# Two-layer graph network: 332 single-bucket edge tiles and 50 shared ones in place of 432, and the second layer in the edge loop's block

## Chip, cores, metric

The kernel runs on one core of a Trainium2 chip. The metric is the device time of one execution in microseconds (us). Engines: PE (TensorE), DVE (VectorE), ACT (ScalarE), POOL (GpSimd), SP (SyncE, which here only issues DMAs).

## The reference

1250 nodes with 512 features each, and 41250 directed edges (20000 random pairs in both directions, and one loop per node), sorted by destination. Everything is fp32.

```python
h = relu(layernorm(x))
m = relu(concat(h[src], h[dst]) @ W0.T + b)      # one row of 512 for each edge
x = x + segment_sum(m, src)                      # first layer
h = relu(layernorm(x))
msgs = (h @ W1.T)[src] * edge_weight[:, None]
out = segment_sum(msgs, dst)
x = x + where(out >= 0, out, alpha * out)        # second layer
```

## The kernel before

Nodes are split into ten blocks of 125 (`BN`), so an edge belongs to one of 100 buckets (source block, destination block). A *tile* is 128 edges of one bucket. Since the counts are only known on the chip, the number of tiles is the worst case: `MAXT = (E + 127 * 100) // 128 + 10 = 431`, in groups of four (`GRP`) 108 groups (`NGRP`) and 432 tiles (`NT`). Every engine works through all 432, empty ones too.

**First block: sorting, and the products of layer one.** The edges lie as 125 rows by 330 columns (`EROWS`, `ECOLS`). DVE counts the buckets (`hist`, `tiles_of`, `tile_base`), and in five chunks of 66 columns (`NCHUNK`, `CHUNK`) each edge gets its slot: PE counts by column (`count`), ACT copies the counts out (`copy_counts`), DVE scans them (`bases`), SP writes the sums as extra rows of `hot`, PE makes prefix sums (`prefix`), DVE picks each edge's own (`pick`) and `slots` works out tile, lane and table row. Then each column's edges are put where they belong in one of two ways: 136 columns by an indirect DMA that POOL issues (L374) to a table in DRAM; 194 columns by PE (`place`, L624): three matmuls of a 125x128 one-hot times value (`lane_piece`, by ACT L737 or DVE L459) with a 125x432 one-hot of the tile number (`hot_tile`, DVE L453). Between these columns PE also computes, from a written-out schedule (`STEP`, `TURN_AT`, ...), `a = h @ W0a.T + b` and `b = h @ W0b.T` for all ten blocks, each kept as a rounded high and a low part (`a_hi`, `a_lo`, `b_hi`, `b_lo`). The table is read back (`raw`), added to PE's part, and decoded to `local_s`, `local_d` (node number in its block) and `weight_h`, `weight_l`.

**Second block: the edge loop.** For each tile PE does four matmuls of 512 columns into one `edge_ps` (L994, L995, L999, L1000): `turned_d` with `b_hi`, `b_lo`, and `turned_s` with `a_hi`, `a_lo`. The turned one-hots are made by ACT, a group at a time, from a row that SP broadcasts from DRAM (`spread`): a Square (L1051) and a Relu (L1060). ACT writes `msg_hi` (L1076), DVE `msg_lo` (L1148), and PE sums both over the edges into `node_ps` (`sum_tile`, L955, L956); DVE adds each pair of tiles to `S` (L1129). For layer two the kernel builds a 1250x1250 matrix `M` of summed edge weights: DVE makes `hot_s`, `hot_d` of a group (L1139), POOL multiplies `hot_d` with the high and the low weights (L914), one PE matmul of 252 columns a tile gives a 125x125 block in both parts (`weights`, L966), ACT copies a pair out (L1068), DVE joins the parts (L1134), and POOL adds a block to `M` at an offset read from a table (L930). PE does two sums of an earlier tile behind the four edge matmuls of the next, so ACT and DVE have more than a tile's time. The loops run in turns of four groups (`UNROLL`) with register offsets.

**Third block: layer two.** It starts when all engines have ended the second. SP loads `W1` (L1242), DVE makes the statistics of all ten blocks of `S` (L1275, L1280), PE turns `h2` and `W1` (L1389, L1398), ACT and DVE split them into high and low parts, and PE computes `G = h2 @ W1.T` (ten blocks of 12 matmuls, L1379 to L1381) and `M` times `G` (ten blocks of 30). DVE does the last steps of each block (L1318, L1320, L1323) and SP stores it (L1245).

Of the kernel before, what the change touches and what calls it, by code (L numbers as in the profile page):

```python
# [20 lines left out]
ALU = mybir.AluOpType  # L21
ACT = mybir.ActivationFunctionType
# [22 lines left out]
MAXT = (E + (TILE - 1) * NBKT) // TILE + NBLK * (PAIR - 1)  # L45
NGRP = -(-MAXT // GRP)
NT = NGRP * GRP
# [26 lines left out]


# [3 lines left out]
UNROLL = 4  # L79
KC = D // P  # L80
# [6 lines left out]
assert 2 * NCHUNK == NBLK and (NGRP - 4) % UNROLL == 0 and UNROLL % 2 == 0  # L87


def build(nc, x, src, dst, edge_weight, w0, b0, w1, alpha, out):  # L90
    rows_dram = nc.dram_tensor("edge_rows", [2, NGRP, GRP * P], BF16).ap()
    table_dram = nc.dram_tensor("edge_table", [P * NT, TABLE_FIELDS], F32).ap()
    with ExitStack() as top:
# [8 lines left out]
        iota = sb("iota", [P, NT], F32)  # L102
# [6 lines left out]
        shift = sb("shift", [P, NBLK], F32)  # L109

# [5 lines left out]
        local_d = sb("local_d", [P, NT], F32)  # L116
        weight_h = sb("weight_h", [P, NT], F32R)
# [5 lines left out]
        with ExitStack() as early:  # L123
# [17 lines left out]
            tile_base = early_sb("tile_base", [EROWS, NBKT], F32)  # L141
            blk_small = early_sb("blk_small", [EROWS, 6, NBLK], F32)
# [11 lines left out]
        with ExitStack() as scope:  # L154
# [4 lines left out]
            digit_room = sb1("digit_room", [P, (2 * NBLK * ECOLS * 2 - 4 * NT * 4 - 2 * NGRP * (GRP + 2) * 4) // 4 + 32], F32)  # L159
# [14 lines left out]
            with ExitStack() as ranks:  # L174
                hot = sb1("hot", [EROWS + 2, NBKT, CHUNK], BF16, ranks)
            with ExitStack() as back:
                raw = sb1("raw", [P, NT, TABLE_FIELDS], F32, back)
                code = sb1("code", [P, NT], F32, back)
                spare = sb1("spare", [P, NT], F32, back)
                started = sb1("started", [NBKT, NT], F32, back)  # L180
            hot_room = sb1("hot_room", [P, NBKT * CHUNK], BF16)
            weight_all = raw[:, :, W_AT]
            iota_h = sb1("iota_h", [EROWS, P], F16)
# [11 lines left out]
            row_no = sb1("row_no", [EROWS, ECOLS], I32)  # L195
            bkt_small = sb1("bkt_small", [NBKT, 8], F32)
# [48 lines left out]
            carried = sem("carried")  # L245
            rows_in = sem("rows_in")
# [4 lines left out]
            slot_math = sem("slot_math")  # L251
# [26 lines left out]
            with nc.Block() as block:  # L278
                @block.sync
                def _(sp):  # L280
# [11 lines left out]
                    sp.dma_start(table_dram.rearrange("(p t) f -> p (t f)", p=P),  # L292
                                 zeros.rearrange("p t f -> p (t f)")).then_inc(cleared_dram, 16)
                    for k in range(NCHUNK):
                        for r, part in enumerate((base_hi, base_lo)):
                            sp.wait_ge(base_rows, 2 * k + r + 1)
                            sp.dma_start(hot[EROWS + r:EROWS + r + 1].rearrange("p (s d) c -> p s (d c)", s=NBLK),
                                         part.rearrange("s d c -> s (d c)")).then_inc(rows_in, 16)

                    for k in range(2):  # L300
# [3 lines left out]
                                 table_dram.rearrange("(p t) f -> p (t f)", p=P)).then_inc(table_in, 16)  # L304
# [4 lines left out]
                def _(pool):  # L309
# [7 lines left out]
                    pool.iota(iota[:], [[1, NT]], base=0, channel_multiplier=0,  # L317
# [65 lines left out]
                def _(dve):  # L383
# [46 lines left out]
                    def slots(k):  # L430
                        cols = slice(k * CHUNK, (k + 1) * CHUNK)
                        whole = planes[:, 0, :]
                        dve.wait_ge(picked, (k + 1) * NPICK)
                        dve.tensor_reduce(slot[:], planes.rearrange("p b c -> p c b"), AX.X, ALU.add).then_inc(slot_math, 1)
                        dve.wait_ge(slot_math, k * 4 + 1)
                        dve.tensor_scalar(whole, slot[:], -(TILE - 1) / 2, 1.0 / TILE, ALU.add, ALU.mult).then_inc(slot_math, 1)
                        dve.wait_ge(slot_math, k * 4 + 2)
                        dve.tensor_scalar(tile_no[:, k % 2, :], whole, MAGIC, -MAGIC, ALU.add, ALU.add).then_inc(slot_math, 1)
                        dve.wait_ge(slot_math, k * 4 + 3)
                        dve.scalar_tensor_tensor(out=lane[:, k % 2, :], in0=tile_no[:, k % 2, :], scalar=-float(TILE), in1=slot[:],  # L440
                                                 op0=ALU.mult, op1=ALU.add).then_inc(slot_math, 1)
                        dve.wait_ge(slot_math, k * 4 + 4)
                        dve.scalar_tensor_tensor(out=row_no[:, cols], in0=lane[:, k % 2, :], scalar=float(NT),
                                                 in1=tile_no[:, k % 2, :], op0=ALU.mult, op1=ALU.add).then_inc(slots_ready, 1)

                    def column(q):
# [6 lines left out]
                        dve.tensor_scalar(hot_tile[r][:], iota[0:EROWS, :], tile_no[:, k % 2, at:at + 1], None, ALU.is_equal)  # L453
                        if KINDS[k][at] == "A":
                            dve.tensor_scalar(hot_lane[r][:], iota_h[:], lane[:, k % 2, at:at + 1], None,  # L455
# [33 lines left out]

                    dve.wait_ge(dconst, 3)  # L490
# [8 lines left out]
                    dve.tensor_copy(iota_h[:], iota[0:EROWS, 0:P])  # L499
# [3 lines left out]
                    own(dve.tensor_scalar(zt[:], total_ps, (TILE - 1) / 2, 1.0 / TILE, ALU.add, ALU.mult))  # L503
                    own(dve.tensor_scalar(tiles_of[:], zt[:], MAGIC, -MAGIC, ALU.add, ALU.add))

# [4 lines left out]
                    own(dve.tensor_tensor_scan(pair_to, ones_row[:, 0:NBLK], pair_a, 0.0, ALU.mult, ALU.add))  # L510
# [10 lines left out]


                    own(dve.tensor_tensor(own_base[:], by_blk[0:NBLK],
# [5 lines left out]
                    for s in range(5, NBLK):  # L529
                        hot_of_block(0, s)  # L530
# [916 lines left out]
```

## Time before and its profile

| what | value |
|---|---|
| median of three runs | 1081.85 us (1081.13 to 1082.65) |
| the profiled execution: its time | 1083.92 us |
| the profiled execution: its span | 1082.2 us |
| granted TensorE clock, mean over the span | 0.987 |
| PE busy | 1023.7 us (95%), 4879 matmuls |
| DVE, ACT, POOL busy | 949.4, 836.0, 716.6 us |

The span is from the first to the last instruction, and the time is 1.7 us longer. Busy time of PE counts pipelined matmuls that overlap, so the distance between the starts of two matmuls is the better measure of its work.

### The profile page before, as it was taken

How to read it: one execution, taken by the hardware profiler on the slowest of the kernel's cores; microseconds unless marked ns; L12 is line 12 of the kernel's file. 1: busy time of each engine (PE TensorE's matmuls, PEld its weight loads, DVE VectorE, ACT ScalarE, POOL GpSimd, SP SyncE). 2: the span in 40 equal slices, each digit the busy share in tenths (PEclk: the TensorE clock that was granted, in tenths of full speed). 3: DMA queues.
4: the chain of work that ended last, by engine and by line, in shares of the span. 5: the costliest groups of instructions: out<-in, count | busy, mean ns of one | idle time of the engine just before them, and what ended most of it. 6: DMA issues, size and time to landing. Idle time of an engine off the chain costs nothing. (4 is left out here: it accounts for less than half of the span.)

```text
span 1082.2 us, 22605 instructions
## 1 busy us (share of the span) xinstructions
PE 1023.7 (95%) x4879; PEld 814.1 (75%) x4880; DVE 949.4 (88%) x1801; ACT 836.0 (77%) x1769; POOL 716.6 (66%) x1042
## 2 busy tenths in 40 slices
PE   5698999999799999999999999999999999959997
PEld 4386887777588788777888777777778877748775
DVE  7798899888599999999999999999999999973454
ACT  6777798788688888888888888888888888844210
POOL 3888787867567777777777777777777777730000
PEclk9999999999899999999999999999999999979999
DMA  7000000000111111111111111111111111010011
GB/s 209 2 2 3 2 3 2 4 2 2 54 44 43 42 43 39 43 41 41 44 38 43 42 43 43 38 43 42 42 43 38 43 42 42 25 39 1 20 34 42
DMA packets 37249, 38.15 MB, mean 35 GB/s; under 512 B 5990, under 2 KB 33431, under 8 KB 37212
## 3 DMA queue, kind: packets, MB, share of 16 engines
q1 hardware_dynamic: 32512, 37.07, 11.0%
q0 software_dynamic: 4416, 0.30, 1.6%
q8 instruction: 18, 0.29, 0.1%
q10 hardware_dynamic: 284, 0.33, 0.1%
q14 instruction: 19, 0.16, 0.0%
HBM read 34.04 MB, written 3.36 MB: 35 GB/s over the span
## 5 line engine op out<-in xcount | busy, mean ns | idle before, releaser
L1076 ACT ACTIVATE msg_hi<-edge_ps 128x512 fp32r<-128x512 f32 x432 | 257.8, 597 | 81.7 <-PE edge_ps L1000 81.7
L930 POOL TENSOR_TENSOR M<-M,pair_w 125x125 f32 x432 | 210.9, 488 | 162.0 <-DVE pair_w L1134 122.5
L1148 DVE SCALAR_TENSOR_TENSOR msg_lo<-edge_ps,msg_hi 128x512 fp32r<-128x512 f32 x432 | 290.8, 683 | 20.7 <-ACT msg_hi L1076 15.1
L374 POOL DMA_INDIRECT edge_table<-fields,row_no x136 | 176.7, 1299 | 50.3 <-issue 40.5
L914 POOL TENSOR_TENSOR hot_w<-hot_d,weight_l 128x252 fp32r<-128x252 bf16 x216 | 180.8, 837 | 0.0
L737 ACT ACTIVATE lane_piece<-hot_lane,fields 125x128 fp32r<-125x128 bf16 x498 | 155.6, 391 | 30.6 <-DVE hot_lane L455 30.2
L955 PE MATMUL node_ps<-msg_hi,hot_s 128*125 128x512 f32 x432 | 176.5, 409 | 0.2 <-DVE msg_lo L1148 0.2
L994 PE MATMUL edge_ps<-b_hi,turned_d 125*128 x432 | 172.8, 400 | 1.3 <-ACT turned_d L1060 0.7
L624 PE MATMUL psum<-hot_tile,lane_piece 125*128 125x432 f32 x582 | 157.2, 394 | 16.5 <-ACT lane_piece L737 16.3
L999 PE MATMUL edge_ps<-a_hi,turned_s 125*128 x432 | 171.4, 397 | 0.1
L995 PE MATMUL edge_ps<-b_lo,turned_d 125*128 x432 | 171.3, 397 | 0.0
L1000 PE MATMUL edge_ps<-a_lo,turned_s 125*128 x432 | 170.7, 395 | 0.0
L956 PE MATMUL node_ps<-msg_lo,hot_s 128*125 128x512 f32 x432 | 170.5, 395 | 0.0
L1051 ACT ACTIVATE square<-spread,minus_no 125x512 f32<-125x512 bf16 x214 | 154.0, 719 | 3.5
L1129 DVE TENSOR_TENSOR S<-S,node_ps 125x512 f32 x216 | 146.7, 679 | 1.9
L624 PEld LDWEIGHTS psum<-hot_tile,lane_piece 125*128 125x128 f32 x582 | 109.0, 195 | 39.9 <-ACT lane_piece L737 21.4
L914 POOL TENSOR_TENSOR hot_w<-hot_d,weight_h 128x252 fp32r<-128x252 bf16 x216 | 131.5, 609 | 4.0 <-DVE hot_d L1139 3.1
L1068 ACT COPY pair_w<-m_ps 125x504 f32<-125x504 f32 x216 | 123.2, 571 | 4.1 <-POOL M L930 4.0
L1134 DVE TENSOR_TENSOR pair_w<-pair_w 125x252 f32<-125x252 f32 x216 | 111.1, 514 | 2.5 <-ACT pair_w L1068 2.5
L955 PEld LDWEIGHTS node_ps<-msg_hi,hot_s 128*125 128x125 f32 x432 | 80.3, 186 | 36.1 <-issue 18.5
L453 DVE TENSOR_SCALAR hot_tile<-iota,tile_no 125x432 fp32r<-125x432 f32 x194 | 96.1, 496 | 10.3 <-PE psum L624 9.9
L966 PEld LDWEIGHTS m_ps<-hot_w,hot_s 128*125 128x125 f32 x432 | 79.1, 186 | 24.0 <-POOL hot_w L914 2.6
(206 smaller groups left out, 1726.6 us busy)
## 6 DMA issues: line engine op xcount, KB each, us to landing
spread<-edge_rows SPq DMA_DIRECT2D x214, 125.0 KB
out_dram<-result SPq DMA_DIRECT2D x10, 250.0 KB
edge_table<-fields,row_no POOLq DMA_INDIRECT x136, 2.6
w_in<-in_L_gnn_W_dram SPq DMA_DIRECT2D x1, 2048.0 KB, 11.6
S<-in_x_dram SPq DMA_DIRECT2D x1, 1792.0 KB
w_in<-in_L_gnn_W_dram SPq DMA_DIRECT2D x1, 1024.0 KB, 5.2
S<-in_x_dram SPq DMA_DIRECT2D x1, 448.0 KB
edge_table<-zeros SPq DMA_DIRECT2D x1, 432.0 KB, 15.3
```

The source lines that it names most:

```text
L374: pool.indirect_dma_start(table_dram[:, :], bass.IndirectOffsetOnAxis(ap=row_no[:, c:c + 1], axis=0), fields[:, c, 0:TABLE_FIELDS], None). ...
L624: mm = pe.matmul(code_ps if f == 0 else weight_ps, lane_piece[r][:, f, :], hot_tile[r][:], start=(q == 0 and f < 2), stop=True, skip_group ...
L914: pool.tensor_tensor(hot_w[h][:, :, f, :], hot_d[k][:, h * PAIR:(h + 1) * PAIR, :], part[:, bass.ds(g * GRP + h * PAIR, PAIR)].unsqueeze(2 ...
L930: pool.tensor_tensor(part, part, pair_w[h][:, j, 0, 0:BN], ALU.add).then_inc(m_added, 1)
L955: pe.matmul(sums[:], hot_s[k][:, j, 0:BN], msg_hi[j][:], start=(j % PAIR == 0), stop=False)
L956: pe.matmul(sums[:], hot_s[k][:, j, 0:BN], msg_lo[j][:], start=False, stop=(j % PAIR == PAIR - 1)).then_inc(tile_summed, 1)
L994: pe.matmul(edge_ps[j][:], td, b_hi[:, b_rows], start=True, stop=False)
L995: pe.matmul(edge_ps[j][:], td, b_lo[:, b_rows], start=False, stop=False)
L999: pe.matmul(edge_ps[j][:], ts, a_hi[:, a_rows], start=False, stop=False)
L1000: pe.matmul(edge_ps[j][:], ts, a_lo[:, a_rows], start=False, stop=True).then_inc(edge_ready, 1)
L1076: act.activation(msg_hi[j][:], edge_ps[j][:], ACT.Relu).then_inc(hi_ready, 1)
L1148: dve.scalar_tensor_tensor(out=msg_lo[j][:], in0=edge_ps[j][:], scalar=0.0, in1=msg_hi[j][:].bitcast(F32), op0=ALU.max, op1=ALU.subtract). ...
```

## The change

- An edge tile is now *pure* (one bucket) or *mixed*. Two neighbouring destination blocks of one source block share one mixed tile, 50 in all (`NMIX`), one for each pair of buckets, and it takes what is left over of both. The number of pure tiles falls to `(41250 // 128 + 10)` rounded up to 83 groups: 332 (`PURE`). The tables have 52 + 332 = 384 columns (`NT`) in place of 432.
- A mixed tile needs both destination blocks: six edge matmuls in place of four (`turned_o` is the one-hot of the second block, with `b` of that block), a third Square and Relu on ACT for each group, a third set of one-hots on DVE (`local_o`), twice the products on POOL, and two weight matmuls in place of one, accumulating into one bank (`weights_mixed`). DVE adds that bank straight to two blocks of `M` (`add_mixed`); ACT's copy and POOL's additions are gone. Offsets are constants, and the 50 tiles are written out without a loop. Sums of five tiles go to one block of `S` (`add_block`).
- The first block finds the mixed tile in `slots`, which has 12 small operations in place of 5; a third row of `hot` carries the mixed tile's start, loaded once; the code of an edge gets one more bit. `count` stands four columns further ahead in a chunk and `copy_counts` before the end of the chunk (`COUNT_BACK`, `COPY_BACK`).
- `make_hots` reads an fp16 `iota_h` in place of the fp32 `iota`; `square` is bf16.
- Layer two stands in the block of the edge loop. Statistics of a block of `S` are made between mixed tiles, `W1` is loaded once the last edge matmul has read the space, the first turns and products stand behind the last tiles, and each result is stored in two DMAs of 112 and 13 rows in place of one of 125.

```diff
-MAXT = (E + (TILE - 1) * NBKT) // TILE + NBLK * (PAIR - 1)
-NGRP = -(-MAXT // GRP)
-NT = NGRP * GRP
+NBP = NBLK // 2
+NMIX = NBLK * NBP
+MGRP = -(-NMIX // GRP)
+MIXC = MGRP * GRP
+NGRP = -(-(E // TILE + NBLK * (PAIR - 1)) // GRP)
+PURE = NGRP * GRP
+NT = MIXC + PURE
...
                     def slots(k):
...
+                        own(dve.tensor_reduce(slot[:], planes.rearrange("p b c -> p c b"), AX.X, ALU.add))
+                        own(dve.tensor_scalar(quotient, slot[:], -MID_SLOT, 1.0 / UPPER, ALU.add, ALU.mult))
+                        own(dve.tensor_scalar(upper, quotient, MAGIC, -MAGIC, ALU.add, ALU.add))
+                        own(dve.scalar_tensor_tensor(out=slot[:], in0=upper, scalar=-UPPER, in1=slot[:], op0=ALU.mult, op1=ALU.add))
+                        own(dve.tensor_scalar(quotient, slot[:], -(TILE - 1) / 2, 1.0 / TILE, ALU.add, ALU.mult))
+                        own(dve.tensor_scalar(whole, quotient, MAGIC, -MAGIC, ALU.add, ALU.add))
+
+                        own(dve.tensor_tensor(after, whole, upper, ALU.subtract))
+                        dve.scalar_tensor_tensor(out=at, in0=whole, scalar=-float(TILE), in1=slot[:], op0=ALU.mult, op1=ALU.add)
+                        dve.tensor_scalar(in_mix[:], after, float(MID_TILE), None, ALU.is_equal)
+                        own(dve.scalar_tensor_tensor(out=tile, in0=after, scalar=float(MID_TILE), in1=whole, op0=ALU.is_le, op1=ALU.add))
+                        own(dve.copy_predicated(tile, in_mix[:].bitcast(U16), mix_no[:, cols]))
...
+                for h in range(2):
+                    weigh_mixed(h)
                     add_weights(NGRP - 1, h)
+                for m in range(2, NMIX):
+                    weigh_mixed(m)
...
+                for m in range(NMIX):
+                    edges_mixed(m)
+                    if m < 2:
+                        sum_tile(NGRP - 1, PAIR + m, (NGRP - 1) % 2)
+                    else:
+                        sum_mixed(m - 2)
+                    if m in (1, 3):
+                        weights(NGRP - 1, (NGRP - 1) % 2, m // 2)
+                    if m >= GRP:
+                        weights_mixed(m - GRP)
+                for m in range(NMIX - 2, NMIX):
+                    sum_mixed(m)
...
+                weights_mixed(NMIX - 4)
+                turn_h(0)
+                weights_mixed(NMIX - 3)
+
+                pe.wait_ge(node_added, NGRP * 2 + NBLK)
+                turn_h(1)
+                weights_mixed(NMIX - 2)
+                weights_mixed(NMIX - 1)
+                pe.wait_ge(w1_loaded, 16)
+                for i in range(KC):
+                    turn_w1(i)
...
-                    return dve.tensor_tensor(hot[:], iota[:, 1:1 + OHW].unsqueeze(1).to_broadcast([P, GRP, OHW]),
...
+                    return dve.tensor_tensor(hot, iota_h[:, 1:1 + OHW].unsqueeze(1).to_broadcast([P, GRP, OHW]),
...
+                        if j == 2 and u + 1 < MGRP:
+
+                            if u == 0:
+                                dve.wait_ge(hots_w, NGRP * 4)
+                            else:
+                                dve.wait_ge(mix_weighed, u * 2 * GRP)
+                            hots_of_mixed(u + 1)
```

## Rows read from the trace of the kernel before

**Rows 1.** Windows: us; busy of PE, PEld, DVE, ACT, POOL; clock; DMA; GB/s.
```profile
42.60:278.40 235.80, 223.08 (x1222) 178.96 (x1222) 204.17 (x536) 184.90 (x563) 175.87 (x136) 1.00 0.08 5
294.00:952.30 658.30, 657.72 (x2997) 526.42 (x2996) 644.24 (x1069) 575.06 (x1066) 497.76 (x848) 1.00 0.13 41
600.00:800.00 200.00, 200.00 (x911) 159.06 (x910) 196.44 (x326) 174.68 (x325) 151.47 (x262) 1.00 0.13 42
952.30:971.90 19.60, 7.11 (x37) 5.82 (x35) 14.39 (x36) 7.65 (x14) 6.15 (x13) 0.74 0.17 54
971.90:1002.20 30.30, 30.30 (x141) 24.42 (x142) 10.44 (x18) 14.32 (x24) 0.00 (x0) 0.94 0.01 1
...
1005.70:1075.60 69.90, 69.87 (x300) 55.51 (x300) 32.33 (x37) 11.19 (x10) 0.00 (x0) 1.00 0.11 33
```

**Rows 2.** Timeline of PE in the edge loop: start us, us, instruction.
```profile
500.12 0.40 PE L966 MATMUL m_ps<-hot_w,hot_s 128*125 128x252 f32 x2
500.35 0.39 PE L994 MATMUL edge_ps<-b_hi,turned_d 125*128 x1
...
502.68 0.39 PE L955 MATMUL node_ps<-msg_hi,hot_s 128*125 128x512 f32 x1
```

**Rows 3.** Groups by form, 310 to 960 us: busy us, mean ns; idle before.
```profile
L1148 DVE SCALAR_TENSOR_TENSOR msg_lo<-edge_ps,msg_hi 128x512 fp32r<-128x512 f32 x420 | 282.5, 683 | 11.3 <-ACT msg_hi L1076 5.7
L1076 ACT ACTIVATE msg_hi<-edge_ps 128x512 fp32r<-128x512 f32 x419 | 250.1, 597 | 77.3 <-PE edge_ps L1000 77.3
L930 POOL TENSOR_TENSOR M<-M,pair_w 125x125 f32 x427 | 208.4, 488 | 156.8 <-DVE pair_w L1134 117.8 <-POOL M L930 37.7 <-PE m_ps L966 1.3
L914 POOL TENSOR_TENSOR hot_w<-hot_d,weight_l 128x252 fp32r<-128x252 bf16 x211 | 177.4, 841 | 0.0
...
L1051 ACT ACTIVATE square<-spread,minus_no 125x512 f32<-125x512 bf16 x207 | 148.9, 719 | 3.4
L1129 DVE TENSOR_TENSOR S<-S,node_ps 125x512 f32 x211 | 143.3, 679 | 1.8
L914 POOL TENSOR_TENSOR hot_w<-hot_d,weight_h 128x252 fp32r<-128x252 bf16 x211 | 128.1, 607 | 0.0
...
L1139 DVE TENSOR_TENSOR hot_s<-iota,local_s 128x504 fp32r<-128x504 f32 x104 | 87.0, 837 | 0.0
...
L1060 ACT ACTIVATE turned_s<-square 125x512 fp32r<-125x512 f32 x104 | 66.8, 642 | 0.0
```

**Rows 4.** Waits, 39 to 280 us: us in total, times, longest.
```profile
ACT lane_piece L737 <- DVE hot_lane L455: 30.2, 35, 4.1
...
DVE counts L403 <- ACT counts L726: 10.9, 4, 3.6
...
DVE hot_tile L453 <- PE psum L624: 9.9, 17, 2.4
```

**Rows 5.** Timeline of DVE in the first block.
```profile
230.61 0.20 DVE L436 TENSOR_SCALAR planes<-slot 125x66 f32<-125x66 f32 x1
230.85 0.20 DVE L438 TENSOR_SCALAR tile_no<-planes 125x66 f32<-125x66 f32 x1
...
268.52 0.43 DVE L453 TENSOR_SCALAR hot_tile<-iota,tile_no 125x432 fp32r<-125x432 f32 x1
268.88 0.23 DVE L455 TENSOR_SCALAR hot_lane<-iota_h,lane 125x128 bf16<-125x128 f16 x1
```

**Rows 6.** Timeline between the edge loop and layer two.
```profile
961.23 0.41 SPq L1242 DMA_DIRECT2D w_in<-in_L_gnn_W_dram  x1
...
971.90 0.79 PE L1379 MATMUL psum<-w1T_hi,h2T_hi 128*125 128x512 f32 x1 [2.35 <-DVE w1T_lo L1261]
```

**Rows 7.** The page: one group, and one DMA issue with its landing time.
```profile
L374 POOL DMA_INDIRECT edge_table<-fields,row_no x136 | 176.7, 1299 | 50.3 <-issue 40.5
...
w_in<-in_L_gnn_W_dram SPq DMA_DIRECT2D x1, 1024.0 KB, 5.2
```

**Rows 8.** Waits of the DMA queue's own engine, whole span.
```profile
SPq L1247 <- DMA out_dram<-result: 3.7, 1, 3.7
```

More of the change, by code:

```diff
@@ L436, in slots @@
[L436 to L441, printed above, removed]
@@ new lines, in sum_mixed @@
+                def sum_mixed(m):
+                    u, j = divmod(m, GRP)
+                    s, p = divmod(m, NBP)
+                    k = (NGRP + u) % 2
+                    pe.wait_ge(lo_ready, PURE + m + 1)
+                    pe.matmul(node_ps[s % 2][:], hot_s[k][:, j, 0:BN], msg_hi[j][:], start=p == 0, stop=False)
+                    pe.matmul(node_ps[s % 2][:], hot_s[k][:, j, 0:BN], msg_lo[j][:], start=False,
+                              stop=p == NBP - 1).then_inc(tile_summed, 1)
@@ new lines, in weights_mixed @@
+                def weights_mixed(m):
+                    u, j = divmod(m, GRP)
+                    h, k = m % 2, (NGRP + u) % 2
+                    pe.wait_ge(mix_weighed, 2 * m + 2)
+                    if m < 2:
+                        pe.wait_ge(m_copied, NGRP * 2 - 1 + h)
+                    else:
+                        pe.wait_ge(mix_added, m - 1)
+                    for f in range(2):
+                        mm = pe.matmul(m_ps[h][:, 0], hot_s[k][:, j, 0:BN], hot_w[h][:, f], start=f == 0, stop=f == 1)
+                    mm.then_inc(mix_ps, 1)
@@ new lines, in product, with turn_h @@
+                def product(ps, stationary, moving, first, last):
+                    pe.matmul(ps, stationary[0], moving[0], start=first, stop=False)
+                    pe.matmul(ps, stationary[1], moving[0], start=False, stop=False)
+                    return pe.matmul(ps, stationary[0], moving[1], start=False, stop=last)
+                def turn_h(b):
+                    pe.wait_ge(h2_ready, b + 1)
+                    if b >= 2:
+                        pe.wait_ge(h2_lo, b - 1)
+                    for c in range(KC):
+                        mm = pe.transpose(psum[:, 4 + b % 2, c * BN:(c + 1) * BN], h2[b % 2][:, c * P:(c + 1) * P],
+                                          ident[0:BN, 0:BN])
+                    mm.then_inc(h2_ps, 1)
@@ new lines, in _, with rest @@
+                for g in range(REST, NGRP):
+                    group(g, g % 2, last=g == NGRP - 1)
+                def rest(b):
+                    lo, hi = BATCHES[b]
+                    dve.wait_ge(std3, b + 1)
+                    dve.reciprocal(rstd[0:BN, lo:hi], std[:, lo:hi]).then_inc(rstd3, 1)
+                    dve.wait_ge(rstd3, 2 * b + 1)
+                    dve.scalar_tensor_tensor(out=shift[0:BN, lo:hi], in0=mv[:, lo:hi, 0], scalar=-1.0,
+                                             in1=rstd[0:BN, lo:hi], op0=ALU.mult, op1=ALU.mult).then_inc(rstd3, 1)
@@ new lines, in _ @@
+                for u in range(MGRP):
+                    mixed(u)
+                    if u == 9:
+                        rest(0)
+                add_block(NBLK - 1)
+                stats_of_block(NBLK - 1)
+                rest(1)
+                moments_of((NBLK - 1,))
+                add_mixed(NMIX - 5)
+                low_of_h2(0)
+                add_mixed(NMIX - 4)
+                add_mixed(NMIX - 3)
+                low_of_h2(1)
+                rest(2)
+                add_mixed(NMIX - 2)
@@ L1424, in build @@
+        tail.close()
         scope_m.close()
```

710 lines of the change are left out of this document (426 added, 284 removed).

## The prediction

> **What bounds the kernel.** I read the windows first, then the timeline of PE, the groups of the loop, and the waits. The windows [rows 1] show four stretches. From 294 to 952.3 us, 61% of the span, PE is busy all the time. DVE is busy 196.4 of 200 us beside it, so PE leads by little. From 952.3 to 971.9 PE is busy 7.1 of 19.6 us: the edge loop has ended and layer two has not begun. Behind it PE is full again. From 42.6 to 278.4 no engine is full: PE 223, DVE 204, ACT 185 of 236 us, and each waits for the others in turn [rows 4]. So a tile less is worth its PE time, the gap at 952.3 is worth its length, and the first block has to be read by its waits.
>
> PE's work is measured by distances between starts [rows 2]. From 500.35 to 502.68 ten matmuls of 512 columns start, so one takes 0.233 us; two of 252 take 500.35 - 500.12 = 0.23 together, 0.116 each. A tile has six of the first and one of the second: 1.51 us. The window gives 911 matmuls in 200 us, at 7 a tile 130.1 tiles, 1.537 us each. The 0.02 more is the change of turn.
>
> **Tiles.** Before: 432 x 1.537 = 664.0 us. After: 332 x 1.537 = 510.3. A mixed tile has eight matmuls of 512 and two of 252: 8 x 0.233 + 2 x 0.116 = 2.10 us, times 50 = 104.8. Sum 615.1, so **-48.9 us**, if PE stays the bound.
>
> The Trainium skill, "TensorE: Matmul & The Clock Gate", Back-to-back issue gap, gives N/2.4 + 2.5 ns between matmuls, 216 ns for 512 columns. With it a pure tile is 1.40 us, a mixed one 1.94 and the term -43 us, an estimate. This trace has 233 ns, and the trace decides.
>
> Does PE stay the bound in the mixed tiles? Per four of them (8.4 us of PE), from [rows 3]:
> - ACT: four msg_hi (0.60) and three pairs of Square and Relu (0.72 + 0.64) are 6.5 us. Hidden. But `turned_o` has one buffer: its Relu stands behind the msg_hi of the fourth tile, so it is ready some 0.4 (a matmul's duration [rows 2]) + 0.5 (msg_hi less its overlap) + 0.64 + 0.1 = 1.65 us after the last edge matmul of that tile starts, and PE needs it after that matmul, two sums, two weight matmuls and four edge matmuls, 1.86 us. It just fits; I charge 1 us in all, 0 to 6.
> - POOL: eight products (0.61 and 0.84 in turns) are 5.8 us. Hidden.
> - DVE: four msg_lo (0.68), three one-hots (0.84 by hot_s), four add_mixed of 250 columns (no row; half an L1129 and no less than a third: 0.3 to 0.4), 0.8 additions to `S` and 0.8 statistics (both as L1129), are 2.7 + 2.5 + 1.4 + 1.1 = 7.7 us. Durations overlap by almost 0.1 us each, so about 6.8. Hidden, with the least to spare.
>
> **Hand-over from pure to mixed.** POOL's order is: products of tile 0, additions of the last pure group's first half, products of tile 1, additions of its second half, products of tile 2. The second half is joined by DVE only behind msg_lo of mixed tile 5, some 5 x 2.1 + 2.0 + 1.0 = 13.5 us after the first mixed tile begins. Then come two additions (1.2 with their gaps) and the products of tile 2 (1.45): ready at 16.1. PE wants them behind the sums in tile 6, at 6 x 2.1 + 1.9 = 14.5. So PE waits 1.6 us; behind it queue only PE's own edges. With ACT's extra one-hots in the last pure group (6.9 us of work for 6.1) I take **+2 us** (0 to 5), and with `turned_o` +3.
>
> **First block.** On the path to the first placed column DVE has more to do. A small dependent operation costs 230.85 - 230.61 = 0.24 us [rows 5]. Five more in the tile arithmetic are 1.2, three for the mixed row 1.2 (one is 660 wide), two for the code 1.2 (330 wide), seven in slots 1.7: +5.3. The DMA of the third row lands while DVE still makes one-hots and codes. The four later slots: 4 x 7 x 0.24 = +6.7. Against this: `count` and `copy_counts` stand earlier, so the waits of DVE for counts go, three of four: 10.9 - 3.6 = -7.3 [rows 4]. `hot_tile` has 48 columns less; its distance is 0.36 us for 432 columns [rows 5], so 0.025 to 0.04 us each, 194 times: -5 to -8, I take -6. PE's placing matmuls shrink by 48 x 0.454 ns = 22 ns, 582 times 12.7 us, but DVE waited for PE only 9.9 us in all [rows 4], and PE for ACT: I take -3. Sum 5.3 + 6.7 - 7.3 - 6 - 3 = -4.3, I take **-4**. Bounds: nothing gained gives +12. The other side is held by POOL: its 136 scatters need 176.7 + 40.5 = 217.2 us [rows 7], begin at about 42 + 5, and end at 264; landing and reading back add some 6, so no earlier than 270 where it is 278.4: -8. The decode has four more operations and narrower ones: **+1**.
>
> **From the last edge matmul to the first product of G.** Before: 19.6 us [rows 1, 6], 952.3 to 971.9, in which SP issues the load of W1 only at 961.2, behind the barrier. After, with T the end of the last edge matmul: the load is issued at T and lands at T + 5.5 [rows 7]. DVE and PE have their own chain: msg_hi, msg_lo, sums to T + 2; addition of the last block, its statistics and small operations to T + 4.6; then by turns weight matmuls, `add_mixed` and low parts of h2, to about T + 8; then the first low part of W1. First product at T + 9, so **-10.6 us**. Bounds: the load alone, T + 7.5, and a chain in which every step costs half as much again, T + 13. The clock: at 952.3 to 971.9 PE was idle for most of the time and the granted clock was 0.74 and then 0.94 of the 2.4 GHz level [rows 1]; PE is idle less now, worth up to 6% of 30.3 = 1.8 us. I take 0.
>
> The products of layer two (30.3, 3.5 and 69.9 us) stay. The last store took 3.7 us from issue to landing [rows 8] for 250 KB, where 1024 KB landed in 5.2 [rows 7]; at that rate its data need 1.3, so 2.4 could go, and a second issue costs some 0.5. I take **-1** (+0.5 to -2.4). The Trainium skill, "DMA: Bandwidth & Descriptors", Why a DMA increments its semaphore by 16 and not by 1, says a DMA uses the largest number of engines up to 16 that divides its rows: 5 for 125 rows, 16 for 112. By that the -1 is an estimate to be believed; no row here shows the engines.
>
> **Sum.** -48.9 + 3 - 4 + 1 - 10.6 - 1 = -60.5 us. The profiled execution took 1083.9 us, so 1023.4 as its like; the median of the runs is 2.1 us under it, so 1021 to 1022. I say **1022 us**.
>
> **Rivals.**
> - *DVE becomes the bound in the mixed tiles.* With full durations DVE needs 7.7 us for four, and its waits (mix_weighed for one-hots, mix_ps for additions) come on top. At 2.5 us a tile instead of 2.1 the end is 20 us later: 1042. For it: DVE is at 98% already in the pure loop [rows 1]. Against: it loses the join, and its share there was reached at 1.54 us a tile. Chance 0.18.
> - *The first block gets longer.* The added operations are on DVE, on whose one-hots ACT waited 30.2 us [rows 4]; if the earlier counts and narrower columns give nothing, the block is 12 us longer rather than 4 shorter: 1038. Chance 0.17.
> - *More than the sum.* The first block gains its full 8, the clock 2, tail 2, hand-over 0: 1010 or less. Chance 0.10.
> - *Slower than before.* The one-hots of the pure loop read a 2-byte iota from an odd element, beside 4-byte operands. No row shows this form. DVE has 3.6 us in 200 to spare, 0.11 us in a group of 6.15. Two one-hots a group (0.84): if each took x more, the loop would grow by 83 (2x - 0.11). It eats the 60.5 us at x = 0.42, half as long again; at twice as long (x = 0.84) it costs 130 us: 1152. Against: `hot_lane` reads the same fp16 iota, from element 0 and with a scalar, 128 columns in 0.23 us [rows 5], which is not slow. Chance 0.05.
> - *That the tiles are not fewer* can't be: both counts are constants of the program.
>
> The sum as forecast has 0.50, between 1012 and 1032. The range for 8 in 10 is 1007 to 1046: it takes in the first-block rival and the DVE rival at 2.5 us, and leaves out 0.06 below and 0.12 above. A measurement of this kernel tells 0.2% (2 us) from no change: faster 0.93, same 0.02, slower 0.05.
>
> **What would show it.** Windows: a pure tile at 1.54 us and a mixed one at 2.1, PE busy in both; a PE idle of about 2 us near the sixth mixed tile, ended by POOL's products; the edge loop beginning 3 us earlier; 9 us from the last edge matmul to the first product; no wait of DVE for counts but the first. The prediction is wrong if mixed tiles take 2.4 or more with PE waiting for msg_lo or one-hots, if the one-hots of the loop are longer than 0.84, or if the first block ends behind 282.

## The result, and the profile after

Median 1024.97 us (4 runs, 1023.95 to 1026.75) against 1082.25 of the kernel before (4 runs, 1081.13 to 1084.27): ratio 0.9471, 95% interval 0.945 to 0.9491. Forecast was 1022. The profiled execution took 1024.19 us, span 1022.5, where the one of before had 1083.9 and 1082.2.

The windows of the changed kernel (us; busy PE, PEld, DVE, ACT, POOL; clock; DMA share; GB/s) are, in this order, the pure tiles, the mixed tiles, the gap before layer two, G's products, and the rest. The clock is the granted one of PE, as a share of 2.4 GHz. They answer to [rows 1].

```profile
289.00:798.00 509.00, 508.59 (x2316) 408.82 (x2317) 493.22 (x822) 446.98 (x828) 389.81 (x648) 1.00 0.13 42
798.00:906.60 108.60, 105.85 (x494) 84.64 (x493) 88.62 (x166) 76.00 (x129) 64.83 (x107) 1.00 0.09 27
906.60:915.40 8.80, 6.35 (x41) 4.88 (x40) 7.48 (x21) 5.10 (x11) 3.55 (x7) 1.00 0.38 119
915.40:945.90 30.50, 30.49 (x148) 24.66 (x149) 12.64 (x20) 16.39 (x28) 0.00 (x0) 1.00 0.01 2
945.90:1022.50 76.60, 71.04 (x306) 56.12 (x304) 35.93 (x41) 11.88 (x11) 0.00 (x0) 0.98 0.11 34
```

Measured between the same instructions in both timelines, the span's -59.7 us are made up like this (about 2.2 us from the last product to the result are alike in both):

| stretch | before | after | difference | forecast |
|---|---|---|---|---|
| start to the first edge matmul | 287.2 | 289.0 | +1.8 | -3 (first block -4, decode +1) |
| edge tiles | 665.0 | 617.7 (509.1 + 108.6) | -47.3 | -45.9 (-48.9 + 3) |
| last edge matmul to the first product of G | 19.75 | 8.8 | -10.95 | -10.6 |
| products | 103.7 | 102.1 | -1.6 | 0 |
| last result to the end | 4.4 | 2.8 | -1.6 | -1 |

Two of these differences are not the change's alone. The unchanged first block of the changed kernel was profiled seven times in all (this profile and those of runs 1, 2, 3, 5, 6 and 11), and its first edge matmul began at 289.0, 293.5, 291.1, 292.4, 292.9, 292.7 and 298.3 us; the table has the earliest. And the products took 102.0 us in the second profile of the kernel before (run 7), as long as in the changed one: in its first profile PE had the lower clock for the first of them. The rows are PE's window in the first and in the second profile of before:

```profile
971.90:976.00 4.10, 4.10 (x11) 3.26 (x12) 0.23 (x2) 1.52 (x2) 0.00 (x0) 0.58 0.00 0
```

```profile
971.90:976.00 4.10, 4.07 (x20) 3.32 (x21) 0.60 (x3) 2.49 (x5) 0.00 (x0) 1.00 0.00 0
```

The waits of the mixed stretch (us, times, longest) show what PE loses there in its two longest waits: 1.4 us to POOL, 0.8 to ACT.

```profile
PEld m_ps L1252 <- POOL hot_w L1110: 4.5, 7, 1.8
PE m_ps L1252 <- POOL hot_w L1110: 1.4, 1, 1.4
DVE M L1600 <- POOL M L1083: 1.2, 1, 1.2
PE edge_ps L1230 <- ACT turned_o L1343: 0.8, 1, 0.8
```

PE's timeline has the long wait in the weight matmuls of mixed tile 6, and behind it tiles 2.10 us apart (the second row is the first matmul of tile 7, the last two are those of tiles 12 and 13):

```profile
814.88 0.50 PE L1252 MATMUL m_ps<-hot_w,hot_s 128*125 128x252 f32 x2 [1.40 <-POOL hot_w L1110]
815.22 0.39 PE L1222 MATMUL edge_ps<-b_hi,turned_d 125*128 125x512 f32 x1
...
825.80 0.40 PE L1222 MATMUL edge_ps<-b_hi,turned_d 125*128 125x512 f32 x1
827.90 0.40 PE L1222 MATMUL edge_ps<-b_hi,turned_d 125*128 125x512 f32 x1
```

The one-hots of the pure loop, which one rival made longer, are 772 ns where they were 837 [rows 3]:

```profile
L1511 DVE TENSOR_TENSOR hot_s<-iota_h,local_s 128x504 fp32r<-128x504 f16 x82 | 63.3, 772 | 0.0
```

The first block has lost its waits for counts, as forecast, but ACT waits longer for DVE and DVE no less for PE [rows 4]:

```profile
ACT lane_piece L812 <- DVE hot_lane L495: 41.4, 34, 8.0
...
DVE hot_tile L493 <- PE psum L698: 11.6, 19, 2.3
DVE counts L438 <- ACT counts L801: 3.1, 1, 3.1
```

### The profile page after: what moved, and what is told of

The parts are those of the page before. It is cut to its first block, busy times and chain, and to the rows that moved or that the text cites. A ratio compares the mean times of both kernels' runs of the same rounds, so it can differ in the third digit from the quotient of the medians.

```text
span 1022.5 us, 20099 instructions
## 1 busy us (share of the span) xinstructions
PE 962.6 (94%) x4679; PEld 769.9 (75%) x4680; DVE 889.8 (87%) x1753; ACT 776.2 (76%) x1648; POOL 663.5 (65%) x942
## 4 chain that ended last, share of the span: by engine, by line
PE 68%; DVE 2%; ACT 1%; issue 0%; POOL 0%; POOLq 0%
PE node_ps L1127 8%; PE edge_ps L1166 8%; PE edge_ps L1172 8%; PE edge_ps L1171 7%; PE edge_ps L1167 7%; PE node_ps L1128 7%; PE m_ps L1138 4%; PE psum L1270 3%; PE psum L1272 3%; PE psum L1271 3%; PE m_ps L1252 1%; PE edge_ps L1230 1%; PE edge_ps L1231 1%; PE edge_ps L1227 1%; PE edge_ps L1222 1%; PE edge_ps L1226 1%
## 5 line engine op out<-in xcount | busy, mean ns | idle before, releaser
L1359 ACT ACTIVATE msg_hi<-edge_ps 128x512 fp32r<-128x512 f32 x332 | 198.0, 596 | 59.3 <-PE edge_ps L1172 59.3
L1083 POOL TENSOR_TENSOR M<-M,pair_w 125x125 f32 x332 | 161.2, 485 | 124.3 <-DVE pair_w L1506 94.6
L1520 DVE SCALAR_TENSOR_TENSOR msg_lo<-edge_ps,msg_hi 128x512 fp32r<-128x512 f32 x332 | 224.2, 684 | 17.1 <-ACT msg_hi L1359 12.3
L698 PE MATMUL psum<-hot_tile,lane_piece 125*128 125x384 f32 x582 | 147.2, 375 | 20.6 <-ACT lane_piece L812 19.5
L1127 PE MATMUL node_ps<-msg_hi,hot_s 128*125 128x512 f32 x332 | 134.8, 406 | 0.0
L1166 PE MATMUL edge_ps<-b_hi,turned_d 125*128 x332 | 132.5, 399 | 0.9 <-ACT turned_d L1343 0.7
L1171 PE MATMUL edge_ps<-a_hi,turned_s 125*128 x332 | 131.0, 394 | 0.2 <-ACT turned_s L1343 0.2
L1334 ACT ACTIVATE square<-spread,minus_no 125x512 bf16<-125x512 bf16 x164 | 117.8, 718 | 2.7
L493 DVE TENSOR_SCALAR hot_tile<-iota,tile_no 125x384 fp32r<-125x384 f32 x194 | 91.2, 470 | 11.9 <-PE psum L698 11.6
L1171 PEld LDWEIGHTS edge_ps<-a_hi,turned_s 125*128 125x128 f32 x332 | 62.5, 188 | 15.7 <-issue 0.9
```

What stands on the lines that cost most here:

```text
L698: mm = pe.matmul(code_ps if f == 0 else weight_ps, lane_piece[r][:, f, :], hot_tile[r][:], start=(q == 0 and f < 2), stop=True, skip_group ...
L1083: pool.tensor_tensor(part, part, pair_w[h][:, j, 0, 0:BN], ALU.add).then_inc(m_added, 1)
L1127: pe.matmul(sums[:], hot_s[k][:, j, 0:BN], msg_hi[j][:], start=(j % PAIR == 0), stop=False)
L1166: pe.matmul(edge_ps[j][:], td, b_hi[:, b_rows], start=True, stop=False)
L1171: pe.matmul(edge_ps[j][:], ts, a_hi[:, a_rows], start=False, stop=False)
L1359: act.activation(msg_hi[j][:], edge_ps[j][:], ACT.Relu).then_inc(hi_ready, 1)
```

## The experiments

All start from the changed kernel. They ran on four chips: runs 1, 2, 4 and 5 on one, 6 to 9 on a second, 3, 10 and 11 on a third, 12 on a fourth. The kernel before had medians of 1083.5, 1082.9, 1084.8 and 1082.5 us there. So what follows is read from stretches of the profiles first, and second from ratios, each to the kernel before on the same chip.

**1. The second block's matmuls left out.** Leaves out part of the computation.

```
-                    pe.matmul(ps, turned_s[k][:, at], a_lo[:, source], start=False, stop=False)
-                    if j == 0:
-                        pe.wait_ge(turned, n + 3)
-                    pe.matmul(ps, turned_o[:, at], b_hi[:, second], start=False, stop=False)
-                    pe.matmul(ps, turned_o[:, at], b_lo[:, second], start=False, stop=True).then_inc(edge_ready, 1)
+                    pe.matmul(ps, turned_s[k][:, at], a_lo[:, source], start=False, stop=True).then_inc(edge_ready, 1)
```

> Leaves out of the computation: the two matmuls of each mixed tile that add the second destination block's rows (turned_o), 50 x 2 x 0.233 = 23.3 us of PE; everything else, the one-hots too, stays. Theory (PE sets the pace of the mixed tiles): a mixed tile falls from 2.10 us to what the next engine needs, DVE with 88.6 us busy for 50 tiles, so 1.63 to 1.77 us a tile; the mixed stretch goes from 108.6 us to between 86 and 93, and the kernel is 16 to 22 us under the changed kernel (1025.0), 1003 to 1009. Rival (DVE or a ring of waits sets the pace, and PE only looks full): the stretch stays within 5 us of 108.6 and the kernel at 1020 or more.

Measured: median 1019.8 us, ratio 0.9405 (0.9382 to 0.9428), mixed stretch 100.6 us: 8.0 less, not 15 to 22. 23.3 us of PE bought 8, so the result lies between the theory and its rival. PE was the bound, but by 0.16 us a tile only; at 2.01 us PE waits for the weights. Its window, and two of its waits:

```profile
803.18:903.75 100.57, 85.86 (x395) 64.23 (x394) 89.58 (x166) 73.78 (x129) 67.96 (x108) 1.00 0.09 29
...
PE m_ps L1248 <- DVE M L1596: 9.5, 13, 1.5
PE m_ps L1248 <- POOL hot_w L1110: 4.6, 6, 1.3
```

DVE is busy 89.6 of 100.6 us in it. The expectation's error was to take busy time, from which overlaps are taken out (1.77 us a tile), for what an engine needs. The full durations of DVE's instructions add up to 99.5 us in the changed kernel's mixed stretch and to 101.6 in this one's, 1.99 and 2.03 us a tile, which is the pace found here.

**2. DVE lighter by a quarter of its one-hots.** Leaves out part of the computation.

```
 def hots_of_mixed(v):
-    make_hots(hot_d[(NGRP + v) % 2][:, 1], local_o, v * GRP).then_inc(hots_d, 1)
+    if v < 2:
+        make_hots(hot_d[(NGRP + v) % 2][:, 1], local_o, v * GRP).then_inc(hots_d, 1)
```

> Leaves out of the computation: DVE's one-hots by local_o in 11 of the 13 mixed groups, so that POOL weighs old ones; 11 x 0.75 = 8.3 us of DVE, nothing of PE. Theory (PE sets the pace): the mixed stretch stays 108.6 within 1 us, the kernel 1025 within 1.5. Rival (DVE is the bound or close to it in the mixed tiles): the stretch and the kernel are up to 8.3 us shorter; at 3 us or more DVE is part of the bound.

Measured: mixed stretch 106.7 us, 1.9 less; ratio 0.9498 (0.9477 to 0.9519). Between the two: 1.9 of 8.3 us. Of the 3.6 us by which the 50 tiles exceed 105 (50 x 2.10), about half hang on DVE; the other 105 are PE's.

The distances between the first matmuls of neighbouring tiles show where. The first eight tiles take 19.3 us in the changed kernel and 19.2 here, where 16.8 would be 2.10 each. Behind them the changed kernel has four distances of 2.47 to 2.49 us and one of 2.25; here none is above 2.11. At one of the four, a set of one-hots and the statistics of a block of `S` stand on DVE ahead of the addition to `M` for which PE waits (the changed kernel):

```profile
842.45 0.67 DVE L1511 TENSOR_TENSOR hot_d<-iota_h,local_o 128x504 bf16<-128x504 f16 x1
843.04 0.68 DVE L1586 BATCH_NORM_STATS2 stats<-S 125x6 f32<-125x512 f32 x1
...
844.24 0.40 DVE L1600 TENSOR_TENSOR M<-M,m_ps 125x250 f32<-125x250 f32 x1
...
844.78 0.47 PE L1252 MATMUL m_ps<-hot_w,hot_s 128*125 128x252 f32 x2 [0.15 <-DVE M L1600]
```

**3. Both at once,** to name what stands behind PE.

> Leaves out of the computation: both what the run without the second block left out (the two matmuls with turned_o, 23.3 us of PE) and what the run with a lighter DVE left out (11 sets of one-hots by local_o, 8.3 us of DVE). The first alone took the mixed stretch from 108.6 to 100.6 us, 2.01 us a tile, with PE waiting. Theory (behind PE it is DVE's own work that sets the pace, 2.0 us a tile): with DVE lighter too the stretch falls by most of another 8.3 us, to 92 to 95. Rival (it is a ring of POOL's products, PE's weight matmuls and add_mixed, each waiting for the other two tiles back): the stretch stays at 98 or more.

Measured: mixed stretch 91.3 us; its one execution took 1012.2.

```profile
801.66:892.94 91.28, 84.88 (x394) 64.38 (x393) 80.52 (x154) 73.81 (x129) 62.81 (x108) 1.00 0.11 32
...
PE m_ps L1248 <- POOL hot_w L1110: 3.2, 4, 1.3
PE m_ps L1248 <- DVE M L1599: 2.8, 8, 0.5
```

With PE already light, the stretch falls by 9.3 us from run 1's, as much as DVE's busy time (89.6 to 80.5; the forecast had 8.3), and PE's wait for add_mixed falls from 9.5 to 2.8. So DVE's own work, and not the ring, is the second bound, at 2.01 us a tile.

**4. Two empty pure groups more.** NGRP + 2; MID_SLOT 25600 for the larger table, and a smaller spare room in SBUF.

> Two pure groups (8 tiles, all empty) more, 340 instead of 332. Theory (a pure tile is worth its PE time, 1.537 us before and 1.533 after, whether it holds edges or not): 8 x 1.537 = 12.3 us more in the loop; hot_tile is 8 columns wider, at (0.36 - 0.33) / 48 = 0.0006 us a column and 194 columns placed that is 1.0 us more at most in the first block: +12.3 to +13.3, so 1037 to 1038. Rival (part of the measured difference of the two kernels is not the number of tiles, and a tile is worth clearly less): +10 or less.

Measured: ratio 0.96 (0.9573 to 0.9627), 1039.2 us. Its pure stretch is 522.9 us; five other profiles of the loop with 332 tiles (the changed kernel's and those of runs 1, 2, 5 and 6) had 508.7 to 510.9, so eight tiles are worth 12.0 to 14.2 us, 1.5 to 1.8 each. An empty tile costs about what a full one does (1.53), and the number of tiles is the gain. The medians alone wouldn't settle it: 14.3 us over the changed kernel's first measurement, 9.8 over its second.

**5. W1 loaded late.**

```
-                sp.wait_ge(edge_ready, PURE + NMIX)
+                sp.wait_ge(mix_added, NMIX)
```

> SP issues the load of W1 only behind the last mix_added, where it was issued at the end of the last edge matmul T. Theory (once both chains are short, the load is close to the bound of the gap): issued at T + 7.7 to 8, landed 5.3 later, first product 2.1 behind the landing as now (2.1 from turn_w1 to the first product, 1.2 of waiting for weights_mixed gone): T + 15.1 in place of T + 8.8, so +6.3 us, 1031. Rival (the chain through h2 sets the gap and the load is hidden): within 1 us of 1025.

Measured: gap 17.0 us in place of 8.8, +8.2; ratio 0.9552 (0.9526 to 0.9579), median 1035.2. The load is on the path as said, but 1.9 us are beyond the sum. Of these, 0.7 are the issue, which comes at T + 8.4. The other 1.2 stand between the landing and the first product, 3.3 us in place of 2.1. PE's windows (busy PE, clock, DMA, GB/s) show why: while PE waits for the load the granted clock is at its lower level of 1.2 GHz, and stays there for the transposes of W1. The 16 transposes take 3.67 us there and 1.91 in the changed kernel.

```profile
918.60:924.00 5.40, 0.11 (x1) 0.50 0.59 194
924.00:928.00 4.00, 4.00 (x18) 0.50 0.00 0
928.00:940.00 12.00, 12.00 (x59) 0.99 0.01 2
```

The lower level came without any edit of the gap in run 2 (transposes 3.50 us, gap 9.85), and in runs 8 and 10 too: with this order of instructions the gap is 8.8 at the full clock and 9.8 to 9.9 at half.

**6, 7. Both kernels once more.**

> The changed kernel once more, to see how much its stretches vary from one execution to the next. One theory of where the first block's 5 us went (forecast -4, measured +1.8) is the dependent operations of DVE ahead of the first column, +7.8; a second is mere scatter of the block from run to run: four executions of the same first block so far began the loop at 289.0, 291.1, 292.9 and 293.5 us. Expected: first column at 48.2 to 49.4, loop from 289 to 293.5, mixed stretch 108.6 within 0.3, gap 8.8 within 0.3, from the first product to the end 107.1.

> The kernel before once more, for the same reason. If its first block scatters as the changed one's does, the loop begins between 287 and 292 us, where the profile of before had 287.2; the theory that the first block is truly longer by some 2 us expects it 1 to 3 us ahead of the changed kernel's of the same chip; the rival (no difference but scatter) expects them together.

Measured: the changed kernel 1029.45 us (1027.73 to 1032.7), ratio 0.9516 (0.9497 to 0.9536), the one before 1.0000 (0.9989 to 1.0011). In the changed kernel all stretches behind the first block repeat to 0.2 us (508.9, 108.6, 8.8, 107.1); the loop begins at 292.7 where it was 289.0. In the kernel before it begins at 287.7 where it was 287.2, and the products are 1.6 us shorter, as shown above. So the first block is longer than before, by 2 to 5 us in these pairs and by 11 in the latest of the seven profiles (run 11), and in the changed kernel it scatters. A table of the moments at which the five reductions in slots start, and the decode, from DVE's timelines:

| kernel | slots 0 | 1 | 2 | 3 | 4 | decode |
|---|---|---|---|---|---|---|
| before | 38.4 | 82.6 | 132.9 | 179.7 | 229.6 | 278.4 |
| before again | 38.8 | 82.5 | 132.7 | 178.9 | 228.5 | 278.9 |
| after | 44.9 | 89.3 | 137.7 | 182.9 | 232.6 | 280.3 |
| after again | 45.0 | 89.4 | 140.7 | 186.0 | 236.3 | 284.0 |

The two executions of the same program part between 1 and 2, by 2.9 us. PE in 112 to 120 us, in the first and in the second:

```profile
112.00:120.00 8.00, 8.00 (x38) 1.00 0.08 2
```

```profile
112.00:120.00 8.00, 8.00 (x23) 0.57 0.08 1
```

and in the second's timelines, PE's products at half clock with the prefix behind them, and DVE, which waits for that prefix (in the first execution its wait for the same prefixes is under 1 us):

```profile
118.27 0.63 PE L729 MATMUL psum<-w0T_hi,h1T_hi 128*125 128x512 f32 x1
118.70 0.61 PE L730 MATMUL psum<-w0T_lo,h1T_hi 128*125 128x512 f32 x1
119.12 0.41 PE L731 MATMUL psum<-w0T_hi,h1T_lo 128*125 128x512 f32 x1
119.38 0.36 PE L686 MATMUL psum<-hot,before_b 128*125 128x462 bf16 x1
...
119.77 0.69 DVE L461 COPY_PREDICATED planes<-hot,psum 125x462 f32<-125x462 uint16 x1 [2.88 <-PE psum L686]
```

**8. The counts back in their old places:** COUNT_BACK 2, and copy_counts(k + 1) at the second column of chunk k.

> The matmuls that count, and the copies of the counts, back in their old places (last three columns of a chunk, second column of the next). Theory (the earlier counts took three waits of DVE away, 10.9 - 3.1 = 7.8 us, and these lay on the path of the block): DVE waits for counts four times, about 11 us in all, and the loop begins 5 to 8 us later. Rival (the block is held by a ring of PE, ACT and POOL beside DVE, and the waits were cover for something else): DVE waits again, but the loop begins within 2 us of the changed kernel's.

Measured: DVE waits for counts 9.6 us in four waits (3.1 in one), the decode starts at 288.7 and the loop at 297.4, 4.7 us behind run 6 of the same chip. But the medians are 1031.3 (1028.9 to 1033.7) and 1029.5, ratios 0.9518 and 0.9516, and run 11, with the counts in their new places, has its decode at 289.6 and its loop at 298.3. So the profile's 4.7 us are within the block's own scatter. The waits came back as said; their worth is between 0 and 5 us, and the runs don't settle it. (The edit moves the matmuls by five columns, so they stand five ahead in the changed kernel, not the four named under the change.)

**9. POOL later.**

```
+                    pool.wait_ge(code_ready, 1)
                     for i in range(2 * KC):
                         pool.wait_ge(w_full, i + 1)
```

> POOL begins its eight w0T_lo products only behind code_ready. Theory (DVE's four code operations take 1.24 to 1.45 us each because POOL works beside them): they take about 0.5 us each, the first column comes 3.5 us earlier, at 45, the first scatter some 2 us earlier (POOL ends its own work at about 43), and the loop begins 2 to 3.5 us earlier. Rival (the operations are slow by themselves: 0.79 and 0.97 before, with fp32 and int32 operands): the first column stays within 0.5 us of 48.6.

Measured: first column at 45.00 where it was 48.55, loop from 286.1, earlier than in any profile of the unchanged block; median 1025.96 against 1029.45 on the same chip, ratio 0.9477 (0.9454 to 0.9501). DVE's code operations in the changed kernel, and then in this one:

```profile
28.18 1.24 DVE L598 SCALAR_TENSOR_TENSOR local<-local 125x330 f32<-125x330 f32 x1
29.45 1.45 DVE L600 SCALAR_TENSOR_TENSOR local<-blk,local 125x330 f32<-125x330 bf16 x1
30.94 1.45 DVE L602 SCALAR_TENSOR_TENSOR local<-blk_a,local 125x330 f32<-125x330 f32 x1
32.43 1.42 DVE L604 TENSOR_SCALAR fields<-local 125x330 int32<-125x330 f32 x1
```

```profile
27.40 1.24 DVE L599 SCALAR_TENSOR_TENSOR local<-local 125x330 f32<-125x330 f32 x1
28.67 0.50 DVE L601 SCALAR_TENSOR_TENSOR local<-blk,local 125x330 f32<-125x330 bf16 x1
29.21 0.50 DVE L603 SCALAR_TENSOR_TENSOR local<-blk_a,local 125x330 f32<-125x330 f32 x1
29.75 0.47 DVE L605 TENSOR_SCALAR fields<-local 125x330 int32<-125x330 f32 x1
```

Three operations fall to a third, 2.85 us together. From the start of the first of the four to the first column it is 20.4 us in the changed kernel and 17.6 here, so 2.8 of the 3.55 us are POOL's; the rest was gained ahead of them, where nothing was edited, and is scatter. The first stays at 1.24: POOL's last operation on `fields` still runs beside it. The Trainium skill, "SBUF — State Buffer", Who interferes with whom, says that VectorE and GpSimd share a pair of ports as an exclusive lock: an operation of VectorE with two SBUF inputs blocks while one of GpSimd that reads SBUF has it. The rows agree: DVE's operations start 1.49 us apart (29.45, 30.94, 32.43), and so do POOL's w0T_lo beside them (29.02, 30.50, 31.99, 33.48), which without DVE beside them start 1.23 apart. That sentence of the page doesn't cover the last of the four, which has one SBUF input and fell as much, from 1.42 to 0.47.

**10. PE kept busy in the prologue.** Matmuls of 330 columns into a free bank: 10 ahead of the prefixes, 2 behind each, 14 ahead of the wait for base_out.

> PE gets matmuls of 330 columns that nobody reads, in the prologue only: 10 ahead of the first prefix, 2 behind each of the 15, and 14 ahead of the wait for base_out. Theory (the block's end scatters from 280.3 to 284.9 us, decode's start, because PE idles from 25 to 49 us and then places the first columns at a granted clock of 0.5, as it did in six of the eight profiles of the changed loop so far): the clock is 1.00 from 40 to 70 us, and decode starts at 279.5 to 282, where the changed kernel's second profile had 284.0; the kernel is 2 to 4 us faster than that one's 1029.5. Rival (PE has slack in the block, the clock is no cause): the clock rises, decode still starts at 283 to 285.

Measured: ratio 0.9527 (0.9489 to 0.9566), no gain; first column at 50.5, decode at 289.0. The filling did not reach its aim: the clock is 1.00 from 45 to 50 us, but 0.60 in 50 to 60 and 0.66 in 90 to 100. Run 11, with the prologue as it was, had 1.00 from 40 to 90 us and a decode at 289.6 all the same, and run 6 had 0.50 from 49 to 60 us and the same 44.3 us from slots 0 to slots 1 as the first profile with 1.00. So the level at the start of the block is not what decides. Whether a clock kept up through the whole block would shorten it was not tested.

**11. Three edits in stretches of their own:** POOL's weigh_mixed(2) ahead of the additions of the last pure group's second half; on DVE add_mixed(45) ahead of the last block's addition; one DMA of 125 rows a result.

> Three edits that lie in stretches of their own. (1) POOL weighs mixed tile 2 ahead of the additions of the last pure group's second half: theory (PE's wait in mixed tile 6, 1.40 us, is for these products queued behind the additions) the wait goes and the mixed stretch is 107.0 to 107.4 in place of 108.6; rival (DVE, which waited 1.2 us for POOL's additions, keeps the tile late) 108.3 or more. (2) add_mixed(45) ahead of the last block's addition and statistics on DVE: theory (the last weight matmuls wait for it, and the transposes of W1 stand behind them) the gap is 7.7 to 8.0 in place of 8.8; rival (the delay moves to the statistics and to h2) 8.6 or more. (3) each result is stored by one DMA of 125 rows, as before the change: theory (a DMA of 125 rows is spread over fewer engines) from the last addition to the end it takes 1.6 us more; rival (the gain came from something else) 0.3 or less.

Measured, in one profiled execution (1034.2 us; its loop begins at 298.3): (1) mixed stretch 107.9, 0.7 less; PE's wait in tile 6 is gone and one of 0.80 stands in tile 7, for products of tile 3, now the ones behind the additions. Half of the theory. (2) Gap 8.3, 0.5 less; the weight matmuls now wait for add_mixed(46). (3) 1.5 us more behind the last product. The queue's last wait in the changed kernel and in this one, then the line of DMA share over 40 slices (1018 to 1023 us, and 1026 to 1033):

```profile
SPq L1047 <- DMA out_dram<-result: 1.5, 1, 1.5
...
DMA  0000000000000000000049997893100000000000
```

```profile
SPq L1046 <- DMA out_dram<-result: 3.6, 1, 3.6
...
DMA  0000000000000000333323413223331100000000
```

With 125 rows the share is 0.3 of 16 engines, with 112 it is 0.9. The Trainium skill, "DMA: Bandwidth & Descriptors", Why a DMA increments its semaphore by 16 and not by 1, gives 5 of 16 and 16 of 16 engines, 0.31 and 1; the trace agrees.

**12. What gained, together:** the edits of run 9 and (1) of run 11, and DVE's order add_mixed(45), last block's addition, add_mixed(46), (47), low part of h2, statistics.

> The three edits that gained in their stretches, together: POOL's w0T_lo behind code_ready, POOL's products of mixed tile 2 ahead of the last pure group's additions, and on DVE add_mixed(45) ahead of the last block's addition, now with 46 and 47 right behind it and the statistics after them. Theory: first column at 45.0; mixed stretch 107.9; gap 7.6 to 8.0 where the granted clock is full, limited by the landing of W1; the block's later part scatters as before with the granted clock, so the loop begins between 286 and 291. Sum against the changed kernel -3.6 - 0.7 - 1.0 = -5.3 us: 1020 to 1024, ratio to the kernel before 0.942 to 0.947. Rival (what is gained ahead of the first column is lost in the block again, as its columns wait for each other): the ratio is within 0.002 of the changed kernel's 0.9516 on this measure, 1027 or more.

Measured: 1025.49 us (1021.54 to 1029.43), ratio 0.9477 (0.945 to 0.9504), where the changed kernel had 0.9516 and, first, 0.9471: outside the theory's 0.942 to 0.947 and outside the rival's too. First column at 45.7, mixed stretch 107.8, loop from 288.0, gap 8.4: now the transposes of W1 begin at the landing (910.97, 5.2 us after the issue), and the first product waits 1.14 us for the low part of W1, with two additions to M ahead of it on DVE. Against the repeated run it gains 0.4%; against the first measurement nothing. Two measurements of the same changed kernel differ as much as this gain, so only the stretches show it.

## Why the prediction came out

- **Tiles, -48.9.** Right. A pure tile is 1.533 us (509.06 / 332), a mixed one 2.10 by PE, which is again 0.233 us a matmul. Run 4 puts a pure tile at 1.5 to 1.8 us. The issue gap of the Trainium skill, "TensorE: Matmul & The Clock Gate", 216 ns, would have made the term -43. The page gives it for a single matmul, and for a stream of weight loads and matmuls some 131 ns; this trace, with a weight load ahead of each matmul, shows 233 and neither of them.
- **Hand-over +2, turned_o +1.** The two waits are right in place and nearly in size: the one for POOL's products came in tile 6 with 1.40 us, turned_o was late by 0.8 in the first tile. They make most of the 2.5 us that the first eight tiles take beyond 2.10 each. That the whole comes out at 3.6 over 105 is in part luck: about 1.9 of it hangs on DVE at a few later tiles (run 2), for which the prediction had nothing.
- **DVE as the bound (0.18).** Didn't happen, but was nearer than the working said: it gave DVE 6.8 us for four tiles with 1.6 to spare; run 1 shows 8.0, 0.4 to spare. Subtracting 0.1 for each overlap was wrong: the full durations, 7.7 by the forecast and 8.0 as measured (99.5 us for 50 tiles), are the pace.
- **First block, -4 (and decode +1).** This step failed in sign: the loop began 1.8 us later in the profile and 5.5 in the second, where 3 earlier was forecast. The prediction had named its own sign of being wrong, a first block that ends behind 282. The decode starts at 280.3 in the first profile, but at 282.5 to 289.6 in the other six of the same block. Split at the first column: the prologue, +5.3 by the forecast, was +7.8, and run 9 shows 2.8 of that as POOL beside DVE. Behind the first column the forecast had -9.6 (+6.7 - 7.3 - 6 - 3); from there to the decode it is 231.8 and 235.4 us in two executions where before has 237.6 and 237.7, so -5.8 and -2.3, and up to 241.2 in the seven (+3.6).
  - Counts -7.3: the waits went (-7.8), their worth is between 0 and 5 (run 8).
  - Narrower hot_tile -6 against slots +6.7: the distances are 0.33 for 0.36 us, 194 times, but the seven operations in slots took it back, as the sum had it. DVE is busy 207.1 us from its first column to the decode, 205.9 before.
  - PE -3 failed: PE's matmuls are shorter, but DVE waits for PE 11.6 and 13.0 us, where it was 9.9 and 12.4 in the two profiles of before.
  - What took the rest is in part the granted clock: at 112 to 120 us it cost the second execution 2.9 us against the first. In 190 to 200 us it was 0.66 and 0.54 in the two executions of after, 1.00 in both of before; what that cost no run separates. Why the clock falls there now is argued only (PE is idle more: busy 215.3 of 237 us from 49 to 286 in the first execution, before 219.3; in the second pair it is 218.3 and 220.0); run 10 tried to hold it and did not. Where the block's remaining scatter comes from stays open.
- **Gap, -10.6.** Right: 8.8 for 9. Both chains end nearly together: the load lands 5.3 us after its issue, and the weights of the last tile keep W1's transposes 1.2 us longer.
- **Clock, 0 (bound -1.8).** The products did run at 1.00 from the start and are 1.6 us shorter than in the profile of before, near the bound. But the shorter gap is not shown to be the cause: in the second profile of before, with its gap of 19.7 us, they ran at 1.00 too and took 102.0 us. Taking 0 was right as far as the runs show.
- **Last store, -1.** -1.6, by run 11 the work of the 112 rows.
- **Slower by the fp16 iota (0.05).** Refuted: 772 ns for 837 with hot_s, and 712 for 700 with hot_d.

The total agrees to 3 us in the first measurement and to 7 in the second. Part of that is luck: in the profile the first block's miss (4.8 us) is mostly covered by tiles, products and store, of which 1.6 us is the slow start of the products in that one profile of before, and the block itself was at its shortest.

## What to carry to other kernels

Where one engine is full, its matmuls can be counted, and the count holds to a per cent. In a stretch where no engine is full, terms don't add up: a shorter instruction on one engine buys little where another sets the pace. To see which engine comes second, take work from the first and then from both. Busy shares put its pace 12% too low here, and the sum of its full durations put it right to 1%. Profile both kernels more than once before a difference of a few us is called the change's: here one profile of before had 1.6 us of lower clock, and the changed first block varied by 9 us.

## What the runs showed of the hardware

- DVE operations of 0.50 us took 1.45 beside POOL (run 9). POOL's third operation on `fields` took 3.80 us where the same had 1.06 before, but the first took 0.78 where it had 3.60: which one is held up depends on when DVE's stand beside it.
- At the lower of the clock's levels, for 4 us after PE had idled 6.3 us, 16 transposes took 3.67 us in place of 1.91 (run 5). In the same program this level comes in one execution and not in the next: it moved the first block by 2.9 us (run 6), and the products of before by 1.6 (run 7).
- A store of 125 rows reached 82 to 105 GB/s in most slices of its time, one of 112 rows mostly 262 to 279 (run 11 and the changed kernel).
